# Two-layer graph attention on one core: W2's products with the last layer's vectors moved, the next W1's first rows rounded earlier, the columns' product inside a row block

## The reference, cut to what matters

```python
def gat_layer(x, W, a_s, a_d, b, edge_index, concat):
    h = (x @ W).reshape(n, H, C)
    alpha_s = einsum('nhc,hc->nh', h, a_s); alpha_d = einsum('nhc,hc->nh', h, a_d)
    e = leaky_relu(alpha_s[src] + alpha_d[dst], 0.2)
    e = exp(e - segment_max(e, dst)[dst])
    alpha = e / (segment_sum(e, dst)[dst] + 1e-16)
    return segment_sum(h[src] * alpha[:, :, None], dst) + b
h = elu(gat_layer(x, W1, a_src1, a_dst1, b1))     # 8 heads of 768
out = layernorm(x + gat_layer(h, W2, a_src2, a_dst2, b2))   # 1 head of 768
```

## Time and profile before

| | before |
|---|---|
| median of 3 runs | 645.24 us (645.22 to 646.35) |
| profiled execution | 646.89 us, of which the span from first to last instruction is 645.1 us |
| PE busy | 631.8 us, 98% of the span, 3378 matmuls |
| DVE busy | 538.0 us, 83% |
| ACT busy | 337.5 us, 52% |
| POOL busy | 209.5 us, 32% |
| mean granted TensorE clock | 0.999 of full speed |

### The profile page before, as it was taken

How to read it: one execution, slowest core, us unless ns; L and a number is a source line. 1 busy time by engine, 2 the same in 40 slices (tenths; PEclk the granted TensorE clock), 3 DMA queues, 4 the chain that set the end, 5 groups by cost and what they waited for, 6 DMA issues and landing times.

```text
span 645.1 us, 9269 instructions
## 1 busy us (share of the span) xinstructions
PE 631.8 (98%) x3378; PEld 538.6 (83%) x3378; DVE 538.0 (83%) x960; ACT 337.5 (52%) x570; POOL 209.5 (32%) x133
## 2 busy tenths in 40 slices
PE   9999999999999999999999999989999899999996
PEld 5766568989888898989898989978898789887885
DVE  8999997889979877768676968797789868898976
ACT  7899982536534744553444535253544444533382
POOL 2000000140643824085406740474116540351230
PEclk9999999999999999999999999999999999999999
DMA  9322502125144323051304320450215230500002
GB/s 323 152 75 75 167 6 99 49 60 186 53 144 161 110 99 98 1 186 59 99 1 130 115 75 0 144 175 24 74 47 199 74 99 0 196 26 0 1 2 98
DMA packets 22172, 59.34 MB, mean 92 GB/s; under 512 B 2544, under 2 KB 2800, under 8 KB 22128
## 3 DMA queue, kind: packets, MB, share of 16 engines
q1 hardware_dynamic: 21984, 58.69, 27.6%
q10 hardware_dynamic: 144, 0.07, 0.0%
HBM read 54.03 MB, written 4.72 MB: 91 GB/s over the span
## 4 chain that ended last, share of the span: by engine, by line
PE 82%; DVE 13%; issue 3%; ACT 2%; DMA 0%; DVEq 0%; ACTq 0%
PE O L1378 22%; PE R L1268 9%; PE R L1274 9%; PE R L1271 9%; PE O L1285 7%; PE R L1345 6%; PE R L1351 6%; PE R L1348 6%; DVE L L875 2%; DVE ohd L726 1%; DVE junk L785 1%; DVE junk L766 1%; DVE L L869 1%; DVE y L880 1%; PE O L1345 1%
## 5 line engine op out<-in xcount | busy, mean ns | idle before, releaser
L1182 POOL TENSOR_TENSOR W2l<-Wr,W2h 128x768 fp32r<-128x768 f32 x48 | 91.9, 1936 | 129.2 <-ACT W2h L440 129.2
L1268 PE MATMUL R<-W1h,xTh 128*128 128x384 f32 x312 | 106.7, 342 | 1.8 <-DVE L L869 1.2
L1271 PE MATMUL R<-W1l,xTh 128*128 128x384 f32 x312 | 105.3, 338 | 2.9 <-POOL W1l L1176 2.9
L1274 PE MATMUL R<-W1h,xTl 128*128 128x384 f32 x312 | 105.0, 337 | 0.0
L1186 POOL TENSOR_TENSOR Pl<-L,Ph 128x512 fp32r<-128x512 f32 x34 | 55.2, 1644 | 153.1 <-ACT Ph L491 153.1
L1176 POOL TENSOR_TENSOR W1l<-Wr,W1h 128x768 fp32r<-128x768 f32 x30 | 59.2, 1986 | 130.1 <-ACT W1h L429 129.8
L766 DVE CUSTOM_DVE_ANT_0 junk<-h,abc 128x768 bf16<-128x768 f32 x64 | 67.0, 1047 | 25.6 <-ACT h L452 24.3
L1378 PE MATMUL O<-W2h,gh 128*128 128x256 f32 (+1 forms) x384 | 78.5, 339 | 0.0
L1378 PE MATMUL O<-W2h,gl 128*128 128x256 f32 (+1 forms) x384 | 77.5, 336 | 0.0
L1378 PE MATMUL O<-W2l,gh 128*128 128x256 f32 (+1 forms) x384 | 77.2, 335 | 0.0
L1345 PE MATMUL R<-Ph,hh 128*128 128x512 f32 x168 | 66.2, 394 | 0.0
(11 more groups left out here) (203 smaller groups left out, 1184.2 us busy)
## 6 DMA issues: line engine op xcount, KB each, us to landing
Wr<-in_W SPq DMA_DIRECT2D x101, 384.0 KB, 3.7
abc<-in_as SPq DMA_DIRECT2D x9, 384.0 KB, 5.0
abc<-in_ad SPq DMA_DIRECT2D x9, 384.0 KB, 5.5
h_rows<-h SPq DMA_DIRECT2D x8, 384.0 KB, 2.3
hl<-h_rows SPq DMA_DIRECT2D x8, 384.0 KB, 5.4
xin<-in_xT SPq DMA_DIRECT2D x6, 256.0 KB, 5.8
xr<-in_x SPq DMA_DIRECT2D x1, 1536.0 KB, 6.8
out<-res SPq DMA_DIRECT2D x4, 384.0 KB, 2.3
```

The costliest lines, as they stand in the source:

```text
L1182: e.tensor_tensor(W2l[:, m % N2, :], Wr[:, n, :], W2h[:, m % N2, :].bitcast(f32), ALU.subtract).then_inc(s_w2l, 1)
L1268: e.matmul(bank[:, 0:HALF], xTh[:, f, xs], hi[:, ws], start=f == 0, stop=False)
L1271: e.matmul(bank[:, 0:HALF], xTh[:, f, xs], lo[:, ws], start=False, stop=False)
L1274: m = e.matmul(bank[:, 0:HALF], xTl[:, f, xs], hi[:, ws], start=False, stop=f == FT - 1)
```

## The change

Product k=1 of W2's last rows goes from head 5's place behind `terms` to head 6's place behind `low_h(h, 2)`, and k=4 from head 6's place behind `terms` to head 7's place behind `low_h(h, 2)`. The loads follow the same lists. ACT rounds row blocks 0 and 1 of the next W1 directly behind the last `evict_B`, ahead of `high_h(h, 3)` and `scaled_as`. DVE's first operation of `terms` (adm) goes ahead of the maxima. The columns' product of heads 3 to 6 goes from behind `stage_C(h-1, 2)` to behind the first of its three passes. In head 1 the sources of head 2 go from behind `stage_C(0, 3)` to behind `stage_C(0, 4)`. At the end the first `low_h2` goes ahead of the last step of the last scores.

```diff
--- before.py
+++ after.py
@@ -25,7 +25,7 @@
     EARLY = 3
 
 
-    V_ROWS, V_SCORES = {H - 2: (2,), H - 1: (5,)}, {H - 3: (0, 1), H - 2: (3, 4)}
+    V_ROWS, V_SCORES = {H - 2: (1, 2), H - 1: (4, 5)}, {H - 3: (0,), H - 2: (3,)}
 
     FIRST = 7
     B_AT = [18, 30, 42, 54, 72, 86, 100, 114]
@@ -611,11 +611,11 @@
                     high_h(h, 2)
                     evict_B(h, 3, 0)
                     evict_B(h, 3, 1)
-                    high_h(h, 3)
-                    scaled_as(h, 8 * h + 8)
                     if h + 1 < H:
                         high_w1(h + 1, 0)
                         high_w1(h + 1, 1)
+                    high_h(h, 3)
+                    scaled_as(h, 8 * h + 8)
                     high_w2(h - 1, 4)
                     high_w2(h - 1, 5)
                     scores(h, h, 0, NT, row2, (gl_value(h - 1, FT - 1), (s_g, FT * h)),
@@ -790,8 +790,19 @@
                 e.wait_ge(s_hh, NT * h + t + 1)
                 e.tensor_tensor(hl[:, t, :], hl[:, t, :].bitcast(f32) if 0 < h < EARLY else h32[:, t % 2, :], hh[:, t, :].bitcast(f32), ALU.subtract).then_inc(s_hl, 1)
 
+            by_tile = quad[:, :].unsqueeze(1).broadcast_to([128, NT, 4])
+
+            def by_quarter(a):
+                return a.unsqueeze(2).broadcast_to([128, NT, 4])
+
             def maxima(h, lo, hi, bank):
 
+                if h:
+
+                    if h == 1:
+                        e.wait_ge(s_four, 11)
+                    e.wait_ge(s_asd, 8 * h + 8 if h < H else 8 * H + 1)
+                    e.tensor_tensor(adm[:, :, :], by_quarter(asd[:, h % 2, 1, :]), by_tile, ALU.mult).then_inc(s_adm, 1)
                 for t in range(lo, hi):
                     if t == 0:
                         e.wait_ge(s_bc, bc_value(h, 0))
@@ -814,18 +825,11 @@
                 par = h % 2
                 ad = asd[:, par, 1, lo:hi]
                 n = 2 * h if h < H else 2 * H + lo
-                turned = h > 0
-                by_t, by_b = quad[:, :].unsqueeze(1).broadcast_to([128, NT, 4]), (lambda a: a.unsqueeze(2).broadcast_to([128, NT, 4]))
-                if turned:
-
-                    if h == 1:
-                        e.wait_ge(s_four, 11)
-                    e.tensor_tensor(adm[:, :, :], by_b(ad), by_t, ALU.mult).then_inc(s_adm, 1)
                 e.wait_ge(s_amx, NT * h + hi)
                 e.tensor_tensor(zm[:, lo:hi], amx[:, lo:hi], ad, ALU.add).then_inc(s_zm, 1)
                 e.wait_ge(s_zm, n // 2 + 1)
-                if turned:
-                    e.tensor_tensor(zmm[:, :, :], by_b(zm[:, :]), by_t, ALU.mult).then_inc(s_zmm, 1)
+                if h:
+                    e.tensor_tensor(zmm[:, :, :], by_quarter(zm[:, :]), by_tile, ALU.mult).then_inc(s_zmm, 1)
                     e.wait_ge(s_zmm, h)
                     e.scalar_tensor_tensor(
                         out=mcm[:, :, :], in0=zmm[:, :, :], scalar=SLOPE, in1=zmm[:, :, :], op0=ALU.mult, op1=ALU.max).then_inc(s_mc, 1)
@@ -856,9 +860,11 @@
                     e.wait_ge(*released(RING[RING_AT["r1", h, 0] - 2]))
                 e.transpose(ring_bank("r1", h, 0)[:, :].rearrange("p (c j) -> p c j", j=32), cols[:, 0, :].unsqueeze(2).broadcast_to([128, NT * 4, 32])).then_inc(s_row, 1)
 
-            def scores(h, n, lo, hi, b1k):
+            def scores(h, n, lo, hi, b1k, between=None):
                 d0, d1 = 128 * lo, 128 * hi
                 for u in range(NT + 1):
+                    if between and u == NT:
+                        between()
                     if u < NT:
                         e.wait_ge(s_L, NT * n + u + 1)
                         if u == 0:
@@ -1035,18 +1041,15 @@
                         sums_h(h, t, h32[:, t % 2, :], abc[:, abc_slot(h)[0], :, :])
                         low_h(h, t)
                         if t == 2:
-                            for k in V_ROWS.get(h, ()):
-                                products_W2(k, 8 * h + 6)
+                            for i, k in enumerate(V_ROWS.get(h, ())):
+                                products_W2(k, 0 if i else 8 * h + 6)
                     maxima(h, 0, NT, ring_bank("as", h, 0))
                     terms(h, 0, NT)
                     if h + 3 == H:
                         wait_abc(H)
                     for i, k in enumerate(V_SCORES.get(h, ())):
-                        if i == 1:
-                            rows(h)
                         products_W2(k, 0 if i else 8 * h + 8)
-                    if h not in V_SCORES:
-                        rows(h)
+                    rows(h)
                     scores(h, h, 0, NT, ring_bank("r1", h, 0))
                     sums_P(h)
                     if h == H - 1:
@@ -1103,10 +1106,12 @@
             maxima(H, 0, NT, ring_bank("as", H, 0))
             terms(H, 0, NT)
             rows(H)
-            scores(H, H, 0, NT, ring_bank("r1", H, 0))
-            for t in range(NT):
+            def low_h2(t):
                 e.wait_ge(s_hh, NT * H + t + 1)
                 e.tensor_tensor(hl[:, t, :], res[:, t, :], hh[:, t, :].bitcast(f32), ALU.subtract).then_inc(s_hl8, 1)
+            scores(H, H, 0, NT, ring_bank("r1", H, 0), lambda: low_h2(0))
+            for t in range(1, NT):
+                low_h2(t)
             e.wait_ge(s_P, NT * H + NT)
             for i, to in enumerate((y2, rb)):
                 e.tensor_tensor(to[:, :], L[:, 2 * i, :], L[:, 2 * i + 1, :], ALU.add).then_inc(s_sd, 1)
@@ -1459,13 +1464,17 @@
 
                         for n in range(4):
                             half_B(h + 1, n // 2, n % 2, take("B", h + 1, n))
-                    stage_C(h - 1, c, between=(lambda h=h: denominators(h)) if c == FT - 1 else None,
-                            at=1 if h == H - 1 else 2)
-                    if c == 3 and h == 1:
+                    between = at = None
+                    if c == FT - 1:
+                        between, at = (lambda h=h: denominators(h)), 1 if h == H - 1 else 2
+                    if c == 2 and EARLY <= h < H - 1:
+                        between, at = (lambda h=h: columns(h, take("x", h, 0))), 1
+                    stage_C(h - 1, c, between=between, at=at)
+                    if c == 4 and h == 1:
                         sources(2, 24)
                     if c == 0 and h >= EARLY:
                         sources(h, 8 * h + 8)
-                    if h > 1 and c == (0 if h == 2 else 1 if h == H - 1 else 2):
+                    if (h, c) in ((2, 0), (H - 1, 1)):
                         columns(h, take("x", h, 0))
                 for c in range(FT):
                     stage_A(h, c)
```

## The result

The changed kernel takes 663.02 us, the median of four runs (660.58 to 663.35), against 645.23 us before (also four). The ratio is 1.0263, with a 95% interval of 1.0236 to 1.029. The direction is the forecast one; the size is not: +17.8 us instead of +8.1, and above the end of the range (659).

A forecast was written before the change was run, and what follows sets the result against it. TensorE, busy 631.8 of 645.1 us, bounds the kernel, so only its waits matter. Heads 3 to 6 and small parts: 4.7 + 4.7 - 0.7 + 0.2 - 0.6 - 0.2 = +8.1, giving 653.3 us; own range 651 to 655.5, wider 648.5 to 659.

The forecast's parts named there:

- The losses of heads 5 and 6: TensorE's waits inside `half_B` for W1's low rows and the fourth score, 3.72 and 3.29 us, put down to late scores.
- The early rows make POOL and DVE alternate: Last sums to maxima, heads 3 and 4: queued DVE and POOL operations take turns, rm at 352.5 instead of 347.82.
- 4.2 us and restarts in 0.15: Columns' product, heads 3 and 4: TensorE waits 4.2 us for rm, restarts in 0.15; with 0.3 before, about 4.7 each.
- part 2: The moved columns' product: stands at 347.99 plus 0.3 instead of 350.75 in head 4, so it waits for rm.
- The rival with the clock: Clock falls to 1.2 GHz behind heads 3 and 4's waits, two passes cost 2.8 more each: 658.8 us; chance 0.08.
- 0.3 in head 5: Last part of head 5's loss at the columns' product, 0.3 + 2.4 + 0.3 = 3.0 us.
- Nothing in the trace: Argument against the clock falling behind the long waits: clock stays at 2.4 GHz through the longest wait, 1.45 us.
- head 6's loss of 3.5: Head 6 with four products instead of two before the last sums: loses 3.5 us, net +0.2 after the regained 3.3.
- 0.85: Head 6, before sources: the sums start 0.65 us later, so `sources` waits 0.85 us.
- Come back in full: `half_B` behind heads 5 and 6: earlier scores return the whole 3.7 and 3.3 us.
- head 2's sources: Placed behind one more `stage_C`, they end a TensorE wait of 0.58 us: -0.6.
- The last `low_h2`: First `low_h2` ahead of the last P ends a wait of 0.81: between 0 and -0.8, taken as -0.2 us.

The follow-up runs named there:

- experiment 6: Kernel before with only the products' lists changed (k=1 to head 6, k=4 to head 7, loads to match): 640.35 us, ratio 0.9909.
- Experiment 1: Changed kernel with W1's rows 0 and 1 rounded behind the sums again, all else as changed: 640.58 us, ratio 0.9919.
- experiment 3: Changed kernel with adm behind the maxima again, W1's rows still early and the columns' product still moved: 643.44 us, ratio 0.9956.
- experiment 2: Changed kernel with the columns' product behind the third pass again, W1's rows still early: 647.24 us, ratio 1.0017.
- experiment 8: Changed kernel with both W1's early rows and the moved columns' product undone: 639.18 us, ratio 0.989.
- experiment 4: Changed kernel with overwritten matmuls in front of the columns' product's wait, 16 in heads 3 and 4, 9 in head 5: 654.19 us, ratio 1.0124.
- Experiment 7: Changed kernel with adm behind the maxima again and product k=1 back behind head 5's terms: 643.2 us, ratio 0.9948.

## Why the prediction was wrong

Right were the direction and the mechanism, point by point:

- The losses of heads 5 and 6 were those of late scores, and moving products k=1 and k=4 ends them (experiment 6).
- The early rows make POOL and DVE alternate: second sum, `low_h`, adm and zmm each stood a turn, zm half of one. rm came at 13.98 us after the evict instead of 14.4, and TensorE's wait was 3.99 us instead of 4.2. Experiment 1 removes all of these turns but zm's, which was there before; experiment 3 removes those of adm, zm and zmm. With them go the waits for rm in heads 3 to 5.
- That the long wait of heads 3 and 4 needs all three, the early rows, adm's place and the product's place: with one of them undone it is gone or 1.12 us long (experiments 1, 2 and 3). This does not make two of them free. Against experiment 8 (639.2), the early rows beside adm cost 8.1 us, 7.5 by the spans (experiment 2, 647.2) and the moved product beside adm 1.4 (experiment 1, 640.6). Experiment 2 only looks as good as the kernel before because the products' lists gave 5.5 us back (experiment 6).

The step that failed is the sum's term "4.2 us and restarts in 0.15" of part 2: it left TensorE's clock at its upper level. The rival with the clock had a chance of 0.08 and was what happened. It put the price at 2.8 us for each of heads 3 and 4; measured are 3.00 in head 3, and experiment 4 takes 2.90 of it away. It gave 658.8 us, 4.2 below what was measured. The rival also left out heads 5 and 6, where shorter waits cost clock too. In head 5, 432.03 to 436.65 took 4.62 us for work of 2.90 (1.7 lost), in head 6 1.6 us. Together the clock and the restarts cost some 9.3 us in the four heads. The forecast had 0.15 in each of heads 3 and 4, 0.3 in head 5 and, if head 6's 3.5 was made up in the same way, 0.3 there: 0.9. The difference of 8.4 is the distance between +8.1 forecast and +16.5 in the spans; the other misses nearly cancel. "Nothing in the trace" was no argument against it: the longest wait in the trace was 1.45 us, and the forecast itself made one nearly three times as long.

The second term that was mis-sized is head 6's loss of 3.5, in it the "0.85" for sources. The prediction had the sums issued 0.65 us later, at 478.37; POOL's row, 1.3 us behind ACT's evict (477.21), would have come at 478.5. So the sum's lead was 0.13 us, which the prediction does not say. It was issued 0.90 us later, counted from the head's start, and 0.12 us behind POOL's row, and a turn went the other way: 2.65 instead of 0.85, while the wait for rm fell away. Experiment 7 puts the sum ahead of the row again, and sources no longer waits. "Come back in full" failed for head 6 too: 1.24 us of the 3.29 stayed with the late product k=3. The late sums alone do not explain that: in experiments 3 and 4 sources waits the same 2.49 us, and `half_B` takes 12.58 and 12.57. There product k=3 waits for its load as well, but starts 0.8 to 0.95 us earlier behind sources and stands one turn instead of two. Why the load landed later in the changed kernel stays open.

Small terms: head 2's sources gave 0.86 instead of 0.6. The last `low_h2` gave 0.1 at most instead of 0.2: its wait of 0.81 is gone, and the product behind the sums of P waits 0.70 instead.

## What to carry to other kernels

When a step on one of two engines that exclude each other is moved earlier, list what the other has queued there, and count one whole operation for each queued operation, however small: here 16 columns cost 1.8 us. When a forecast makes an engine wait longer than any wait in the trace, price what comes behind that wait as well. A forecast lead of 0.1 us in such a race decides nothing, and both sides of it belong in the range. And compare a partly undone change with the best of its relatives, not only with the kernel before: a gain from another part can hide a cost of 8 us.

## What the runs showed of the hardware

- DVE's operations with both inputs in SBUF and POOL's subtractions exclude each other for a whole operation (the sum 2.49 us instead of 0.96, zmm 1.74 instead of 0.17) and alternate when both are queued; the maxima, which read PSUM, keep their length (0.68 beside POOL).
- In the profiled executions the granted clock fell to 0.50 behind TensorE's waits of 3.82 and 3.83 us, was 0.64 in the 4.62 us behind the wait of 2.26 us in head 5, and stayed at 1.00 behind waits of 1.45 and 1.12 us and behind experiment 1's 2.05 us (484.21). Behind the same wait of 2.49 us in front of head 6's sources it was 0.51 in the changed kernel, 0.56 and 0.57 in experiments 3 and 4, and 1.00 in experiment 2. The stretches behind that wait, of experiment 2 and then of experiment 4:

```profile
484.31:487.73 3.42, 3.42 (x22) 3.08 (x23) 3.39 (x11) 0.82 (x2) 1.87 (x1) 1.00 0.57 182
```

```profile
490.24:493.66 3.42, 3.42 (x14) 3.03 (x15) 3.39 (x11) 0.82 (x2) 1.82 (x1) 0.57 0.59 170
```

In the same 3.42 us the one holds 22 matmuls and the other 14. The kernel need not be what decides: executions of one kernel differ as well. Of experiment 3's ten, two have a mean granted clock of 0.999 and take 641.9 and 642.04 us, and eight have 0.995 to 0.997 and take 643.12 to 645.76. The kernel before has executions of 645.23 us at 0.999 and of 648.19 at 0.993. Only one execution of each kernel has a trace, so where the clock fell in the others is not known, and what decides was not tried. One or two us between two of these kernels can be the clock's.
